# Metaformer kernel on one core: TensorE turns x for the first norm, later taps load behind the first maps, GpSimd builds all convolution weights

## The reference

```python
qkv = conv1x1(norm(x), w_qkv)                          # norm over the 128 channels of each position
agg = grouped_conv1x1(depthwise_conv5x5(qkv, w_dw), w_pw)
q, k, v = heads(concat(qkv, agg))                      # 16 heads of 3 * 16 channels
q, k = relu(q), relu(k)
out = (q @ (k.T @ [v, 1])) ; out = out[:, :-1] / (out[:, -1:] + 1e-15)
x = x + batchnorm(conv1x1(out, w_proj))
# then: MoE 0 (8 experts, gelu), softmax attention, MoE 1 (16 experts, silu)
```

## Time and profile before

| | |
|---|---|
| median of 3 runs | 446.07 us (444.7 to 447.37) |
| profiled execution | 447.75 us, of which the trace's span is 446.0 us |
| PE busy | 352.9 us, 79% of the span |
| DVE, ACT, POOL busy | 222.9, 210.9 and 178.0 us |
| mean granted TensorE clock | 0.892 of full speed |

### The profile page before, as it was taken

How to read it: one execution, slowest core, us unless ns; L and a number is a source line. 1 busy time by engine, 2 the same in 40 slices (tenths; PEclk the granted TensorE clock), 3 DMA queues, 4 the chain that set the end, 5 groups by cost and what they waited for, 6 DMA issues and landing times.

```text
span 446.0 us, 7931 instructions
## 1 busy us (share of the span) xinstructions
PE 352.9 (79%) x2404; PEld 301.4 (68%) x2404; DVE 222.9 (50%) x565; ACT 210.9 (47%) x554; POOL 178.0 (40%) x202
## 2 busy tenths in 40 slices
PE   3889999997956598957999399898267988977813
PEld 1359999985734598957998265776246888877802
DVE  3618555513675156534776373776841343444306
ACT  4651333333574256734663364566533565554304
POOL 3819554400033655573556000003066555555530
PEclk9999999999896679995999789999665999999875
DMA  7444444324822546310111700000311111111146
GB/s 239 202 74 99 102 96 83 48 37 70 343 73 88 194 176 239 124 49 30 37 38 43 194 2 0 1 1 0 96 42 41 43 43 37 44 36 37 35 119 194
DMA packets 34184, 38.47 MB, mean 86 GB/s; under 512 B 3680, under 2 KB 28640, under 8 KB 33376
## 3 DMA queue, kind: packets, MB, share of 16 engines
q1 hardware_dynamic: 22620, 25.79, 19.8%
q0 software_dynamic: 4096, 8.40, 6.0%
q10 hardware_dynamic: 7428, 3.77, 3.9%
HBM read 24.31 MB, written 7.34 MB: 71 GB/s over the span
## 4 chain that ended last, share of the span: by engine, by line
PE 63%; DMA 8%; DVE 8%; ACT 6%; issue 6%; another core or an unknown queue 5%; ACTq 1%; POOL 1%; SPq 1%; POOLq 0%; DVEq 0%
PE bank L1342 18%; PE bank L1359 12%; PE bank L1252 10%; DMA ln_sq<-y 2%; PE bank L1204 2%; PE bank L1351 2%; PE bank L1424 2%; PE bank L1269 2%; PE bank L1189 2%; ACT w_block L684 2%; PE bank L1383 2%; POOL y L517 1%; PE bank L1133 1%; DMA x_rows<-tok,token 1%
## 5 line engine op out<-in xcount | busy, mean ns | idle before, releaser
L1342 PE MATMUL bank<-x_cols,w_block 128*128 x688 | 104.0, 300 | 20.5 <-ACT w_block L684 9.7
L1342 PEld LDWEIGHTS bank<-x_cols,w_block 128*128 128x128 f32 x688 | 94.1, 212 | 24.5 <-issue 24.3
L510 POOL DMA_INDIRECT x_rows<-tok,token x64 | 60.6, 947 | 65.2 <-DVE dest L970 26.9
L517 POOL DMA_INDIRECT y<-wide,dest x64 | 62.1, 970 | 49.4 <-DVE wide L1046 39.6
L1359 PE MATMUL bank<-w_down,h_cols 128*128 x500 | 75.4, 290 | 4.8 <-DVE wide L1046 3.2
L1359 PEld LDWEIGHTS bank<-w_down,h_cols 128*128 128x128 f32 x500 | 66.9, 203 | 7.3 <-issue 7.0
L1252 PE MATMUL bank<-cmap,cw 128*128 128x112 f32 (+2 forms) x480 | 57.4, 275 | 1.9 <-DMA cmap<-heads 1.9
L1252 PEld LDWEIGHTS bank<-cmap,cw 128*128 128x128 f32 x480 | 55.7, 192 | 3.7 <-DMA cmap<-heads 2.7
L684 ACT ACTIVATE w_block<-w_up 128x512 f32 x86 | 53.6, 623 | 0.9 <-issue 0.9
L321 POOL TENSOR_TENSOR cw<-taps 128x640 f32<-128x640 f32 x24 | 35.7, 1514 | 36.7 <-PE bank L1252 29.5
L1029 DVE TENSOR_TENSOR h_cols<-h_in,bank 128x256 f32<-128x256 f32 x47 | 19.8, 421 | 53.4 <-ACT h_in L701 32.0
(11 more groups left out here) (188 smaller groups left out, 524.8 us busy)
## 6 DMA issues: line engine op xcount, KB each, us to landing
w_up<-in_up_dram SPq DMA_DIRECT2D x4, 1024.0 KB
cmap<-heads SPq DMA_DIRECT2D x48, 64.0 KB
w_up<-in_w_dram SPq DMA_DIRECT2D x1, 2048.0 KB, 7.7
w_down<-in_w_dram SPq DMA_DIRECT2D x1, 2048.0 KB, 13.7
tok<-ln_sq SPq DMA_DIRECT2D x8, 256.0 KB, 2.4
w_down<-in_down_dram SPq DMA_DIRECT2D x4, 512.0 KB
wide<-y SPq DMA_DIRECT2D x8, 256.0 KB, 5.6
ln_sq<-y ACTq DMA_DIRECT2D x8, 256.0 KB, 6.1
```

The costliest lines, as they stand in the source:

```text
L510: pool.indirect_dma_start(out=x_rows[:, j % RING, :], out_offset=None, in_=tok_dram[r], in_offset=bass.IndirectOffsetOnAxis(ap=token[r][:, ...
L517: pool.indirect_dma_start(out=y_dram[r], in_=y_acc[:, s * C:(s + 1) * C], in_offset=None, out_offset=bass.IndirectOffsetOnAxis(ap=dest[r][ ...
L1342: mm = pe.matmul(bank[2 + j % UPS][:, i * 128:(i + 1) * 128], w_block[:, j % 3, i * 128:(i + 1) * 128], x_cols[:, bass.ds(place[j] & ((NB ...
```

## The change

1. The second copy of x is no longer loaded. PE turns each 128x128 block of `xs` into a PSUM bank (`turn_x`, 16 transposes) after two matmuls of no use to the result (`keep_clock(7, 2)`), and DVE takes the statistics from PSUM.
2. Of the four diagonals of a chunk DVE writes two (a `tensor_scalar` from `ident`, in `x_inverse`) and ACT two. ACT's copy of the qkv weights moves behind the first chunk's diagonals.
3. SP issues taps part 3 and `late_w` behind the maps of unit 1, taps part 4 behind those of unit 3.
4. Unit 0 has a semaphore for each map, so PE can start with the first. The last q/k/v heads, `head(2, 0..3)`, move to steps 2 to 5 of the convolution loop (before: two ahead of the loop, two at steps 2 and 3).
5. GpSimd builds all 48 group weights, DVE none. GpSimd's tables `place_id` and `passed` are made after the last weight. DVE's relu of q moves from step 4 to step 8.

```diff
-        def build_weights(engine, u, i):
+        def build_weights(u, i):
...
-                ALU.mult).then_inc(cw_built[i % 2], 1)
+                ALU.mult).then_inc(cw_built, 1)
...
-            xt_load(0)
-            xt_load(1)
-            x_load(0)
...
-            for i, (a, b) in enumerate(TAP_PARTS):
+            for i in range(3):
+                taps_load(i)
...
+                            .then_inc(map_in[n] if n else map_first[g], 16)
+                if n == 1:
+                    taps_load(3)
+                    sp.dma_start(wT[:, W_P0:W_SM + 1, :], late_w).then_inc(w_in, 16)
+                if n == 3:
+                    taps_load(4)
...
             for u in range(len(UNITS)):
-                for i in (0, 2):
-                    build_weights(pool, u, i)
-                if u == CWR - 1:
-                    table(place_id[:, :, :], [[1, 128], [0, 2 * TT]], 0, 0)
+                for i in range(GU):
+                    build_weights(u, i)
                 if u == CWR:
                     table(block_id[:, :, :], [[128, NB], [0, 2 * TT]], 0, 0)
...
-                    for i in range(4):
+                    for i in range(2, 4):
                         act.activation(ln_diag[:, c % 2, i, :], ident[:, :], ACT.Copy,
...
+                if c == 0:
+                    act.wait_ge(wq_mm, 1)
+                    act.activation(wT[:, W_Q:W_V + 1, :], ...
...
-                    dve.bn_stats(x_stat[:, i, :], xc[:, i * 128:(i + 1) * 128]).then_inc(x_stats, 1)
+                    dve.bn_stats(x_stat[:, i, :], bank[c][:, (i % 4) * 128:(i % 4 + 1) * 128]).then_inc(x_stats, 1)
...
                 dve.reciprocal(ln_r[:, 1, 4 * c:4 * c + 4], ln_r[:, 0, 4 * c:4 * c + 4]).then_inc(x_inv, 1)
+                dve.wait_ge(x_inv, c + 1)
+                if c >= 2:
+                    dve.wait_ge(x_spread, c - 1)
+                for i in range(2):
+                    dve.tensor_scalar(ln_diag[:, c % 2, i, :], ident[:, :], ln_r[:, 1, 4 * c + i:4 * c + i + 1], None,
+                                      ALU.mult).then_inc(x_diag[0], 1)
...
-            for u in range(CWR - 1):
-                for i in (1, 3):
-                    build_weights(dve, u, i)
...
-                if s == 4:
+                if s == 8:
                     dve.wait_ge(head_a, 3 * NCH)
...
+            def turn_x(c):
+
+                pe.wait_ge(x_in[c], 16)
+                for i in range(4 * c, 4 * c + 4):
+                    mm = pe.transpose(bank[c][:, (i % 4) * 128:(i % 4 + 1) * 128], xs[:, i * 128:(i + 1) * 128],
+                                      ident[:, :])
+                mm.then_inc(x_turned, 1)
+
+            keep_clock(7, 2)
+            turn_x(0)
+            turn_x(1)
...
-                if s in (2, 3):
-                    head(2, s)
+                if 2 <= s < 2 + NCH:
+                    head(2, s - 2)
```

More of the change, by code:

```diff
@@ L103, with metaformer @@
 TAP_PARTS = [(GT, GT + GU), (GT + GU, GT + 2 * GU), (GT + 2 * GU, 2 * GT), (2 * GT, 3 * GT), (0, GT)]
-def metaformer(nc, x, x_tok, qkv_w, taps_in, late_w, w1, w2, b2, up1, down1, out):
+def metaformer(nc, x, qkv_w, taps_in, late_w, w1, w2, b2, up1, down1, out):
     tok_dram = [nc.dram_tensor(f"tok{r}", (T, C), F32, kind="Internal").ap() for r in range(2)]
@@ L253, in metaformer @@
         kv_ones = sem("kv_ones")
+        map_first = [sem(f"map_first{i}") for i in range(GU)]
         map_in = [sem(f"map_in{u}") for u in range(len(UNITS))]
-        cw_built = [sem("cw_built_pool"), sem("cw_built_dve")]
+        cw_built = sem("cw_built")
         conv_mm, conv_copied = sem("conv_mm"), sem("conv_copied")
@@ L369, in _, with taps_load @@
         def _(sp):
-            def x_load(c):
+            for c in range(NCH):
                 sp.dma_start(chunk(xs, c), chunk(x, c)).then_inc(x_in[c], 16)
-            def xt_load(c):
-                sp.dma_start(chunk(xc, c), chunk(x_tok, c)).then_inc(xt_in[c], 16)
-            xt_load(0)
-            xt_load(1)
-            x_load(0)
[L381 to L385, removed]
-            for i, (a, b) in enumerate(TAP_PARTS):
+            def taps_load(i):
+                a, b = TAP_PARTS[i]
                 sp.dma_start(taps[:, a:b, :], taps_in[:, a:b, :]).then_inc(taps_landed[i], 16)
-                if i == 2:
-                    sp.dma_start(wT[:, W_P0:W_SM + 1, :], late_w).then_inc(w_in, 16)
+            for i in range(3):
+                taps_load(i)
             def rows_store(r):
@@ L486, in _ @@
             for u in range(len(UNITS)):
-                for i in (0, 2):
-                    build_weights(pool, u, i)
-                if u == CWR - 1:
-                    table(place_id[:, :, :], [[1, 128], [0, 2 * TT]], 0, 0)
+                for i in range(GU):
+                    build_weights(u, i)
                 if u == CWR:
                     table(block_id[:, :, :], [[128, NB], [0, 2 * TT]], 0, 0)
[L493 to L498, removed]
+            table(place_id[:, :, :], [[1, 128], [0, 2 * TT]], 0, 0)
+            table(passed[:, :, :], [[128, NI1], [-128, E1 - 1]], 0, 0)
+            pool.wait_ge(tables, E1 + 14)
+            pool.affine_select(out=passed[:, :, :], in_=passed[:, :, :], compare_op=ALU.is_ge, fill=1e6,
+                               base=NB - 1, pattern=[[-1, NI1], [1, E1 - 1]], channel_multiplier=0)\
+                .then_inc(tables, 1)
             def moe_pool(r, E):
@@ L1150, in spread_scale @@
             def spread_scale(c):
-                pe.wait_ge(x_diag, 4 * c + 4)
+                for i in range(2):
+                    pe.wait_ge(x_diag[i], 2 * c + 2)
                 if c >= 3:
@@ L1160, in _ @@
                       start=True, stop=True).then_inc(wq_mm, 1)
+            turn_x(2)
+            turn_x(3)
             for c in range(NCH):
@@ L1481, in _laid_out @@
     return {
-        "x_c": x_c, "x_tok": x_tok, "qkv": qkv, "taps": taps.reshape(128, NG, TAP), "late": late,
+        "x_c": x_c, "qkv": qkv, "taps": taps.reshape(128, NG, TAP), "late": late,
         "w1": w1.transpose(1, 0, 2).reshape(C, E0 * F0),
```

36 lines of the change are left out of this document (16 added, 20 removed).

## The result

The changed kernel takes 460.25 us (median of 4 runs, 458.68 to 462.69), against 446.61 us for the kernel before in the same comparison. The ratio is 1.0317, 95% interval 1.0255 to 1.0379: **slower by 3.2%, 13.6 us, where I had predicted 5.5.** The direction was right, and the time lies above my range. The profiled execution took 461.36 us, its span 459.6.

What follows compares the result with a forecast made beforehand. PE, busy throughout 50 to 90 us in the convolution, bounds the kernel, so a later start counts one for one. Norm 4.1 plus SP's delay 1.4 makes 5.5; on the median 446.07 that gives 451.6 us, range 446.8 to 454.2.

Steps and rivals of the forecast that it cites:

- Part 1: First norm: DVE's diagonal pairs wait for GpSimd's builds, 1.9 us each; last spread at 21.1, H 4.1 later.
- The other terms: First norm, besides the diagonal pairs: two groups of statistics 2.2, three reciprocals 0.6, two scales 1.4 us.
- (b): First norm: one wait a pair, 0.8 instead of 1.9, so H hardly moves; 447.2 us; chance 0.09.
- (c): First norm: DVE's diagonals don't wait for builds, ACT bounds; 446.9 us, or 444.8 without SP's delay; chance 0.13.
- Part 2: From H to PE's first product: three more SP issues make unit 0's sends late; product 1.4 us later after H.
- H: End of the fourth head copy, ahead of the convolution; 21.23 before, forecast at 25.3.
- rival (a): From H to the first product: SP not late, issues hidden, PE keeps its 0.7; 449.5 us; chance 0.16.
- My upper bound of 2.0: From H to the first product: most delay expected, in us, if unit 2's maps are also held up.
- the wait of 2.5 that I forecast: PE's idle time ahead of its first product, some 2.5 us instead of 0.4.
- Part 3: GpSimd's 48 builds, DVE's masks, late tables and the dropped load: costed at nothing, PE covers them.

Runs made afterwards that it cites:

- e2_early_taps: Changed kernel, but taps parts 3 and 4 and late_w are issued ahead of the first map again; ratio to the kernel before 1.0166.
- e4_both: Changed kernel, but ACT writes all four diagonals and taps parts 3, 4 and late_w are issued ahead of the maps; ratio to the kernel before 1.0014.
- e6_hold_early: Changed kernel, GpSimd's builds held until DVE's last diagonal, taps parts 3, 4 and late_w ahead of the maps; ratio to the kernel before 1.0016.
- e3_fill_clock: Changed kernel plus five matmuls of no use to the result ahead of PE's first product; ratio to the kernel before 1.0249.
- b2_late_loads: Kernel before, only three loads moved: taps part 3 and late_w behind unit 1's maps, part 4 behind unit 3's; ratio to the kernel before 1.0144.

## Why the prediction was half right

**Part 1, right in mechanism, a quarter too small.** I took the nearest row, a copy that ended with GpSimd's build and a second that ended with the next one, and priced a pair at 1.9. It costs 2.19 on average, inside my 1.3 to 2.6. The first diagonal does not come at a random point of a build: the work between pairs starts when a build has let go, and where the first waited a whole build (1.28 + 1.30 at 12.41) the pair costs two. That is 4 x 0.29 = 1.2 of the error in the last spread (22.35 against 21.1). The other terms came to 4.2, as summed, though with 0.49 in which DVE waited for ACT's last root (ahead of the reciprocal at 19.69), where I had called ACT no bound. Rivals (b) and (c) are refuted: no second diagonal went ahead, and the builds were there. The Trainium skill's "SBUF — State Buffer", section "Who interferes with whom", says that whoever is first holds the shared ports for the whole instruction and the other is blocked, not slowed. The runs agree: a diagonal takes 0.28 without a build, up to 1.31 beside one, the build unchanged at 1.23.

**Part 2, right in place, wrong in size; this is the step that failed.** The first map arrived at H + 3.3 (3.4 forecast), SP was late by its issues, PE waited for `kvT`; so rival (a) is refuted. But I priced a load's issue at 0.44, the row of a load issued early, when no map had been issued. Among maps it took 0.69 to 0.83, so the three cost 2.4 and not 1.4. And I let the delay of the issue pass on unchanged, as if the way from a send to the product stayed as it was. It grew by 2.5: sends issued and landing more slowly, and ACT's part too. I had seen that the loads travel among the maps, but asked only what that does to maps, not to sends. My upper bound of 2.0 was therefore no bound; 5.1 lay outside it. That the loads' place does this is shown: in the six kernels that have them among the maps on SP the product comes at H + 28.1 to 30.2, in before, e2_early_taps, e4_both and e6_hold_early at H + 25.0 to 26.2. How it slows the landing is not: the second send lands 4.6 to 6.3 after its issue in the six, 4.0 to 5.1 in the four, and these overlap.

**A term that was missing.** I had counted PE's wait at its own length only. At the end of 5.81 us of idle the clock fell to 0.50, and the way to `q_rows` took 3.2 more. The table shows the trend at this place: no low stretch with 0 to 2.2 us of idle, 3.4 us of it with 2.4 and 3.7, 6.8 us with 4.1 to 5.8. e3_fill_clock shows that it is the idle time. The length of one wait doesn't decide alone, though: at the first map b2_late_loads had a low stretch of 3.4 with a wait of 1.92, and the kernel before had none with 1.88. At the wait of 2.5 that I forecast, up to about 1.8 of this could have come as well (e4_both with 2.43 idle; e2_early_taps with 2.16 had no low stretch).

**Part 3, right.** After the change PE never waited for `cw`: all 48 builds lie in its cover, and e4_both and e6_hold_early show that the remaining parts cost nothing measurable.

## What to carry to other kernels

Price a DMA's issue and landing from rows beside the traffic among which it will stand, not from rows ahead of that traffic, and follow the delay through every transfer behind it. Before VectorE instructions such as these `tensor_scalar`s are put beside GpSimd's work, look for rows of the two together, and if they wait as here, count each as one whole GpSimd instruction, or start GpSimd's work after them. A wait of TensorE of several microseconds can cost more than its length: read the granted clock behind it.

## What the runs showed of the hardware

- VectorE diagonals issued back to back let a GpSimd build in between each time: a row of four took 4.43 and 4.96 beside builds, 0.88 without, and the builds kept their 1.23.
- SP's issue of `late_w` took 0.71 to 0.84 between issues of maps, in six kernels, and 0.43 to 0.45 ahead of them, in six others. The issues of the taps parts don't separate so well: 0.59 to 0.89 among maps, 0.43 to 1.49 ahead of them.
- Where the three loads stood among the maps, unit 0's sends on SP had landed 5.4 to 7.1 after the first was issued, in six kernels; where they stood ahead of them, 4.8 to 6.0, in four.
- With TensorE idle for 4.1 to 5.8 us ahead of the first product, the granted clock was 0.50 for 6.8 us, beginning 1 to 3 us ahead of the product.
- The part of the kernel behind `q_rows`, which none of these edits touches, varied between 334.7 and 340.3 us from profile to profile. Differences of under 3 us are told by the ratios alone, not by one profile's span.
